# Attention scores image by image, gate values copied earlier, norm factors in one pass, and other dummy products on TensorE

## What is computed

```
h = concat(cls_tok, tokenizer(x))                    # [64, 6, 256]
h = h + gated_scan(layernorm(h))
h = h + ternary_linear(layernorm(h))
h = h + latent_attention(layernorm(h))
h = h + experts(layernorm(h))                        # 8 experts, top 48 tokens each
```

```
latent = x @ basis_w.T                                        # [B, T, 64]
lt     = einsum('btr,hrs->bhts', latent, head_mats)
att    = einsum('bhts,bus->bhtu', lt, latent) / sqrt(64)
att    = softmax(where(tril, att, -inf))                      # over the T keys of the same image
y      = (att @ v) @ o_w.T + o_b
```

## Time and profile of the kernel before

| | us |
|---|---|
| median of 3 runs | 232.57 (232.18 to 232.72) |
| profiled execution, its own time | 233.47 |
| span of its profile | 231.7 |
| PE busy, PEld busy | 218.0, 172.5 |
| DVE, ACT, POOL busy | 131.9, 73.8, 56.3 |
| mean granted clock of PE | 0.971 |

### The profile page before, as it was taken

How to read it: one execution, slowest core, us unless ns; L and a number is a source line. 1 busy time by engine, 2 the same in 40 slices (tenths; PEclk the granted TensorE clock), 3 DMA queues, 4 the chain that set the end, 5 groups by cost and what they waited for, 6 DMA issues and landing times.

```text
span 231.7 us, 3969 instructions
## 1 busy us (share of the span) xinstructions
PE 218.0 (94%) x1432; PEld 172.5 (74%) x1432; DVE 131.9 (57%) x419; ACT 73.8 (32%) x184; POOL 56.3 (24%) x122
## 2 busy tenths in 40 slices
PE   7999999999969999999999999999797899999995
PEld 5788888889958797778768867978676764655673
DVE  2597657576577475547865664864769525231212
ACT  2124242185676446013411621040036143130310
POOL 1043662266522123020232320300046150000000
PEclk9999999999999999859999997999999799999999
DMA  6999545940000000029999991000001204884002
GB/s 172 345 358 362 207 111 147 433 201 1 3 0 1 3 0 3 0 62 420 429 318 301 422 429 72 3 0 0 3 1 41 78 19 114 340 348 109 0 0 68
DMA packets 9747, 34.31 MB, mean 148 GB/s; under 512 B 1280, under 2 KB 3840, under 8 KB 7424
## 3 DMA queue, kind: packets, MB, share of 16 engines
q1 hardware_dynamic: 9728, 34.07, 40.9%
HBM read 32.88 MB, written 0.39 MB: 144 GB/s over the span
## 4 chain that ended last, share of the span: by engine, by line
PE 77%; DVE 9%; ACT 4%; issue 3%; POOL 3%; DMA 2%; SPq 2%; DVEq 0%; POOLq 0%; ACTq 0%
PE bank L451 16%; PE bank L1040 6%; PE bank L1014 6%; PE bank L676 5%; PE bank L685 5%; PE bank L575 4%; PE bank L600 3%; PE bank L553 3%; PE bank L743 2%; PE bank L440 2%; PE bank L982 2%; PE bank L755 2%; PE bank L463 2%; PE bank L1047 2%; DMA bench<-patches 2%
## 5 line engine op out<-in xcount | busy, mean ns | idle before, releaser
L451 PE MATMUL bank<-desk,bench 118*126 118x256 f32 x190 | 43.9, 381 | 0.2
L451 PEld LDWEIGHTS bank<-desk,bench 118*126 118x126 f32 x190 | 34.6, 188 | 6.2 <-DMA bench<-patches 0.9
L440 PE MATMUL bank<-zeros 128*128 128x256 f32 x94 | 28.2, 424 | 1.1 <-POOL small L1994 1.1
L1999 POOL TENSOR_TENSOR small<-small 96x2 f32<-96x2 f32 (+2 forms) x15 | 9.9, 659 | 70.5 <-DVE small L1312 51.3
L440 PEld LDWEIGHTS bank<-zeros 128*128 128x128 f32 x94 | 17.6, 206 | 3.9 <-POOL small L1994 1.1
L1747 ACT ACTIVATE attic<-bank,cols 128x126 f32<-128x126 f32 x38 | 15.2, 453 | 13.6 <-PE bank L463 13.4
L1094 DVE TENSOR_REDUCE bench<-bench 118x70 f32<-118x630 f32 x19 | 14.7, 798 | 6.5 <-DMA bench<-patches 6.4
L1740 ACT ACTIVATE desk<-bank 126x256 f32<-126x256 f32 x19 | 7.3, 384 | 25.7 <-PE bank L451 22.2
L2007 POOL TENSOR_TENSOR small<-small 126x1 f32<-126x1 f32 x19 | 10.5, 565 | 16.3 <-DVE small L1100 11.6
L685 PE MATMUL bank<-layw,bench 128*96 128x256 f32 x48 | 13.2, 424 | 1.4 <-DVE bench L1421 1.0
L676 PE MATMUL bank<-bench,layw 128*128 128x192 f32 x72 | 13.1, 331 | 0.5 <-ACT bench L1803 0.4
(11 more groups left out here) (220 smaller groups left out, 403.2 us busy)
## 6 DMA issues: line engine op xcount, KB each, us to landing
attic<-experts SPq DMA_DIRECT2D x10, 1024.0 KB, 8.1
desk<-experts SPq DMA_DIRECT2D x6, 1024.0 KB, 15.8
bench<-patches SPq DMA_DIRECT2D x19, 315.0 KB, 4.7
desk<-tokenizer_w SPq DMA_DIRECT2D x4, 576.0 KB, 5.9
layw<-layer_w SPq DMA_DIRECT2D x1, 2184.0 KB, 11.4
attic<-bias SPq DMA_DIRECT2D x8, 256.0 KB, 12.0
cons<-constants SPq DMA_DIRECT2D x1, 1258.0 KB, 5.5
desk<-conv_w SPq DMA_DIRECT2D x5, 128.0 KB, 3.6
```

What stands on the lines that cost most here:

```text
L440: mm(bank[b][:, 0:C], zeros[:, 0:P], zeros[:, :], start=True, stop=True)
L451: i = mm(conv_bank[t % 2][0:TP, 0:C], xt[t % XRING][0:KP, k, :], convw[0:KP, k, :], start=(k == 0), stop=(k == KX - 1))
L1999: pool.tensor_tensor(rs, var, half[0:parts, 0:rs.shape[1]], ALU.pow).then_inc(s(name), 1)
```

## The change

1. Scores image by image. There are 32 products per group, each for one image with its own keys: 48 stationary and 12 moving columns. Even images write partitions 0 to 47, odd ones 64 to 111 (`RH` = 64, `AR` = 112). Mask, softmax and weights have half the columns.
2. POOL makes the second norm's factors for both groups in one pass, `shift_both`. `norm_again` of either group waits for the whole pass.
3. ACT copies `valT` between `norm_again(0)` and `norm_again(1)`.
4. Dummies: one more at each of six places, two fewer at one.

```diff
-AR = 2 * NP2 * T
+RH = 64
+AR = RH + NP2 * T
...
-                        ("causal", 4 * T), ("slots", SW), ...
+                        ("causal", 2 * T), ("slots", SW), ...
...
-        att = [of_group(2 * GT + NP2 * GT + i * 2 * GT, GI // 2, 2, 2, T, parts=AR) for i in range(2)]
+        att = [of_group(2 * GT + NP2 * GT + i * 2 * GT, GI // 2, 2, T, parts=AR) for i in range(2)]
...
-        a_stat = carve(bench, o, 3, IMAGES * 2, parts=AR); o += 6 * IMAGES
+        a_stat = carve(bench, o, 3, IMAGES, parts=AR); o += 3 * IMAGES
...
+        of_image = lambda v, b: v[RH * b:RH * b + NP2 * T]
...
             def att_mask(g):
                 pe.wait_ge(s("lt_dve"), 2 * g + 1)
-                mm(bank[4 * g][0:AR, 0:2 * GT].rearrange("q (i n) -> q i n", n=4 * T), ident[0:AR, 0:AR],
-                   causal.unsqueeze(1).to_broadcast([AR, GI // 2, 4 * T]), start=True, stop=False, skip_group_check=True)
+                mm(bank[4 * g][0:AR, 0:GT].rearrange("q (i n) -> q i n", n=2 * T), ident[0:AR, 0:AR],
+                   causal.unsqueeze(1).to_broadcast([AR, GI // 2, 2 * T]), start=True, stop=False, skip_group_check=True)
...
-                for im in range(0, GI, 2):
-                    i = mm(bank[4 * g][0:AR, im * 2 * T:(im + 2) * 2 * T],
-                           ltT[g][:, im * T:(im + 2) * T, :], latD[g][:, im:im + 2, :, :], start=False, stop=True,
-                           skip_group_check=True)
+                for im in range(GI):
+                    at = im // 2 * 2 * T
+                    i = mm(of_image(bank[4 * g], im % 2)[:, at:at + 2 * T], ltT[g][:, im * T:(im + 1) * T, :],
+                           latD[g][:, im, :, :], start=False, stop=True, skip_group_check=True)
...
             local_back(0)
+            keep_warm(0, 1)
             turn_att(7)
...
             turn_att(8)
-            keep_warm(0, 2)
+            keep_warm(0, 3)
             global_spread(0)
...
             turn_x(0, 0)
+            keep_warm(4, 1)
             local_major(1)
...
             head_products(0)
-            keep_warm(7, 1)
+            keep_warm(7, 2)
             att_mask(0)
             att_scores(0)
             turn_x(1, 1)
             keep_warm(7, 1)
             ternary(1)
-            keep_warm(7, 2)
+            keep_warm(7, 3)
             spread_att(0, 0)
...
             att_scores(1)
             latent_out(0)
-            keep_warm(3, 3)
+            keep_warm(3, 1)
             spread_att(1, 0)
...
             pe.transpose(bank[4][:, 0:E8], cut_row, ident[0:E8, 0:E8]).then_inc(s("cut_turned"), 1)
-            keep_warm(3, 1)
+            keep_warm(3, 2)
...
-                act.wait_ge(s("again"), 5 * (g + 1))
+                act.wait_ge(s("again"), 5)
...
             norm_again(0)
+            act.wait_ge(s("vals_turned"), 1)
+            ac(valT, bank[5][:, 0:UT * E8].rearrange("p (t e) -> p t e", e=E8), ACT.Copy)\
+                .then_inc(s("valT_ready"), 1)
             norm_again(1)
             with_norm(1, 0)
             with_norm(1, 1)
-            act.wait_ge(s("vals_turned"), 1)
-            ac(valT, bank[5][:, 0:UT * E8].rearrange("p (t e) -> p t e", e=E8), ACT.Copy)\
-                .then_inc(s("valT_ready"), 1)
...
+            def shift_both():
+
+                mean, rs, nm = t_mv[0:TR, :, 0], t_rs[0:TR], t_nm[0:TR]
+                for g in range(G):
+                    pool.wait_ge(s(f"t_rs_ready{g}"), 4)
+                pool.tensor_tensor(t_sq[0:TR], rs, rs, ALU.mult).then_inc(s("again"), 1)
+                pool.wait_ge(s("again"), 1)
+                pool.tensor_scalar(t_again[0:TR], t_sq[0:TR], -EPS, 1.0 + EPS, ALU.mult, ALU.add)\
+                    .then_inc(s("again"), 1)
+                pool.wait_ge(s("again"), 2)
+                rsqrt(t_again[0:TR], t_sq[0:TR], "again", parts=TR)
+                pool.wait_ge(s("base_ready"), G)
+                pool.tensor_scalar(nm, mean, -1.0, None, ALU.mult).then_inc(s("nm_ready"), 1)
+                pool.wait_ge(s("again"), 3)
+                pool.tensor_tensor(t_s2[0:TR], rs, t_sq[0:TR], ALU.mult).then_inc(s("again"), 1)
+                pool.wait_ge(s("again"), 4)
+                pool.wait_ge(s("nm_ready"), G + 1)
+                pool.tensor_tensor(t_d2[0:TR], nm, t_s2[0:TR], ALU.mult).then_inc(s("again"), 1)
+                pool.tensor_scalar(t_up[0:TR], rs, 1.0, None, ALU.add).then_inc(s("up_ready"), G)
+                pool.tensor_tensor(t_dn[0:TR], nm, rs, ALU.mult).then_inc(s("shift_ready"), G)
...
-            rs_and_shift(3, 0, 1)
-            rs_and_shift(3, 1, 1)
+            shift_both()
```

More of the change, by code:

```diff
@@ L122 @@
 CONS, CONS_N = offsets([("ident", P), ("headcol", KC * H8), ("mask", TP), ("mask_cut", TP),
-                        ("causal", 4 * T), ("slots", SW), ("spread", 2 * T * P), ("heads8", KC * P), ("mean", P),
+                        ("causal", 2 * T), ("slots", SW), ("spread", 2 * T * P), ("heads8", KC * P), ("mean", P),
                         ("upto", P), ("all", P)])
@@ L1382, in heads_out @@
                                     bank[b][:, 0:2 * GT].rearrange("p (j n) -> p j n", j=2)).then_inc(s("lt_dve"), 1)
-            a3 = lambda i, g: att[i][g].rearrange("q i b p t -> q (i b p) t")
-            st = lambda i, g: a_stat[:, i, g * GI * 2:(g + 1) * GI * 2]
-            bc = lambda v: v.unsqueeze(2).to_broadcast([AR, GI * 2, T])
+            a3 = lambda i, g: att[i][g].rearrange("q i p t -> q (i p) t")
+            st = lambda i, g: a_stat[:, i, g * GI:(g + 1) * GI]
+            bc = lambda v: v.unsqueeze(2).to_broadcast([AR, GI, T])
             def att_shift(g):
-                scored = bank[4 * g][0:AR, 0:2 * GT].rearrange("q (i t) -> q i t", t=T)
+                scored = bank[4 * g][0:AR, 0:GT].rearrange("q (i t) -> q i t", t=T)
                 dve.wait_ge(s("att_scored"), g + 1)
@@ L2077, in rs_tokens, with rs_and_shift @@
                 rsqrt(t_mv[0:TR, sl, 1], t_rs[0:TR, sl], f"t_rs_ready{g}", parts=TR)
[L2079 removed]
+            def rs_and_shift(g):
                 sl = slice(TG * g, TG * (g + 1))
[L2082 to L2088, removed]
[L2089 to L2100 removed]
+                rs_tokens(0, g)
                 pool.tensor_scalar(t_nm[0:TR, sl], t_mv[0:TR, sl, 0], -1.0, None, ALU.mult).then_inc(s("nm_ready"), 1)
[L2102 to L2105 removed]
+                pool.wait_ge(s(f"t_rs_ready{g}"), 1)
+                pool.wait_ge(s("nm_ready"), g + 1)
                 pool.tensor_scalar(t_up[0:TR, sl], t_rs[0:TR, sl], 1.0, None, ALU.add).then_inc(s("up_ready"), 1)
@@ L2192, in _ @@
             probs(9)
-            rs_and_shift(0, 0, 0)
+            rs_and_shift(0)
             rs_local(1)
@@ L2197, in _ @@
             clear_latents(0)
-            rs_and_shift(0, 1, 0)
+            rs_and_shift(1)
             rs_tokens(2, 0)
@@ L2246, in constants @@
     at = np.arange(AR)
-    im, jt = at // (NP2 * T), at % (NP2 * T)
-    late = np.arange(T)[None, None, None] > (jt // NP2)[:, None, None, None]
-    other = np.arange(2)[None, :, None, None] != im[:, None, None, None]
-    causal = np.where(late | other, NEG, np.zeros((1, 1, 2, 1)))
+    im, jt = at // RH, at % RH
+    late = np.arange(T)[None, None] > (jt // NP2)[:, None, None]
+    causal = np.where(late, NEG, np.zeros((1, 2, 1)))
     chan = np.arange(P)
```

18 lines of the change are left out of this document (2 added, 16 removed).

## The result

The changed kernel took 225.65 us in the median of 4 runs (224.99 to 226.44), the kernel before 232.44 beside it (232.18 to 232.72): a ratio of 0.971, with an interval of 0.9675 to 0.9743. That is -6.8 us where -4.6 was forecast. The profiled execution of the changed kernel took 225.71 us.

A forecast was written before the change was run, and what follows sets the result against it. The prediction took TensorE, busy 94% of 231.7 us, as the bound, with three half-clock stretches. Terms -1.6 - 0.1 - 1.1 + 0.4 - 1.8 - 0.8 + 0.4 = -4.6, taken over to the median 232.57: 228.0 us, range 223.8 to 230.9.

The forecast's parts named there:

- all falls go: Rival: every half-clock stretch goes, at 96.6 and 182 us too, -2.2 and -1.5 more, 224.3 us; chance 0.20.
- Scores: Attention scores of both groups: 64 records at 0.030 us, 1.9 us for 2.7, -0.8 per group, -1.6 in all.
- the row of 32 columns: Scores: short weight loads of 32 columns, 0.030 us apart, taken as the price of a record.
- The prediction's own evidence against the rule: Experts' products of 128 rows on two sides of 64 columns: starts 0.01 us apart, 0.59 us both.
- Mask: Mask product of group 0, 192 moving columns for 384: -0.1 us; nothing in group 1, where it is hidden.
- Softmax: Group 1, between scores and spreads: DVE steps of half the size, 0.21 us less each, -1.1 us on the path.
- Ternary at full clock: Behind group 0's scores: the half-clock stretch at 141.0 us goes, ternary 1.74 us for 3.52, -1.8.
- Third dummy behind the ternary: Group 0, ahead of the spreads: one more dummy that no wait covers, +0.4 us.
- Early dummies: Three dummies in waits for DVE at 87 to 105 us: taken as 0, at most 0.1 us each.
- The end: Choosing the expert tokens: the cut row's turn no longer waits for `valT`, -0.8 us; second dummy ahead of the counts, +0.4.
- The clock: Of three places at half clock, the fall at 141.0 us goes, -1.8 us; those at 96.6 and 182.0 aren't counted.
- The slower rival: Scores: short records cost as much as long ones, 0.084 us each, 5.4 us per group, 235.0 us; chance 0.05.

The follow-up runs named there:

- the even-odd order: The changed kernel with the scores of all even images first, then all odd ones; median 233.24 us, ratio 1.002.
- the scores alone: The kernel before with scores image by image, mask and softmax of the change, old dummies and old order; median 227.98 us, ratio 0.986.
- the four variants: The changed kernel without early dummies (226.36 us), with two dummies behind the ternary (226.31), one ahead of the counts (227.83), or all old dummies (226.75).
- the two with filled waits: The changed kernel with two dummies behind the ternary and five more in waits, 225.07 us; the same with one dummy ahead of the counts, 225.07 us.
- one dummy ahead of the counts: The changed kernel with one dummy for two ahead of the counts; 227.83 us, ratio 0.984.

## Why the prediction was right, and where it was off

The direction, the terms of the path and the range held. But the 225.65 us lie nearer to the rival "all falls go" (224.3, with a chance of 0.20) than to the forecast of 228.0 (0.40): the path was right but for the size of the scores, the clock was not.

**Scores: right in kind, mis-sized.** -1.2 and -1.3 per group for -0.8. The sum took 0.030 us a record, from the row of 32 columns; what came is 0.0225 (32 pairs 0.045 us apart, the last with a tail of 0.17), at full clock in both groups:

```profile
135.82 1.61 PE L746 MATMUL bank<-bench 128*48 128x12 f32 x64 [0.21 <-DVE bench L1385]
```

The term that was mis-sized is this price of a record, chosen between two bounds. A pair takes one place of 0.045 us, which is what a single load of 48 columns takes in the even-odd order and is close to the 0.042 that I had by columns. Half of that, with full overlap, was 0.021: I had both figures and then chose a row of another kind because its width was nearer. The loads in the groups of forms:

```profile
L746 PEld LDWEIGHTS bank<-bench 128*48 128x48 f32 x128 | 3.1, 125 | 1.2 <-ACT bench L1845 1.2
```

128 loads are busy 3.1 us in all, at a mean of 125 ns each: most of each load lies over its neighbour. In the even-odd order the same loads, at the same mean, are busy 5.6 us:

```profile
L746 PEld LDWEIGHTS bank<-bench 128*48 128x48 f32 x128 | 5.6, 125 | 1.2 <-ACT bench L1845 1.2
```

The rule of the Trainium skill ("TensorE: Matmul & The Clock Gate", "Part 3: Packing small matmuls"), by which a weight load overlaps running products only where its row group is another one, doesn't hold here: all have 128 rows, and 1.61 us for 2.87, with loads busy 3.1 us for 5.6, is the overlap of two sides. The prediction's own evidence against the rule, was of two products and not of loads, and so was thinner than it said.

**Mask: right.** -0.1.

**Softmax: right.** -1.1 in group 1. The DVE steps took 0.35 us each, as taken:

```profile
L1394 DVE TENSOR_REDUCE bench<-bank 112x32 f32<-112x192 f32 x2 | 0.7, 357 | 3.6 <-PE bank L746 3.6
...
L1402 DVE RECIPROCAL bench<-bench 112x32 f32<-112x32 f32 x2 | 0.7, 354 | 0.1
```

That two dummies had to go for it is shown (+0.6 with three).

**Ternary at full clock: nearly.** 1.97 us for 3.52, -1.55, where the sum took 1.74 and -1.8.

**Third dummy behind the ternary: right.** +0.4, shown at both ends of its interval (5.78 and 5.34).

**Early dummies: right.** Nothing that shows (225.51 without, 225.49 with).

**The end: right.** Turn of the cut row -0.7 for -0.8, since the 0.14 us from the cut row to the turn, which the sum left out, stay; second dummy +0.4. The factors in one pass cost POOL 1.01 us for the power over four columns, and `valT` was copied at 169.56, 3.8 us ahead of the turn:

```profile
168.56 1.09 ACT L1865 ACTIVATE bench<-bench,small 96x256 f32<-96x256 f32 x2 [1.75 <-POOL small L2111]
169.56 0.17 ACT L1965 ACTIVATE small<-bank 128x24 f32<-128x24 f32 x1
...
172.97 0.21 DVE L1669 COPY bench<-small 8x128 f32<-8x128 f32 x1
173.33 0.20 PE L968 MATMUL bank<-cons,bench 8*128 8x8 f32 x1 [0.63 <-DVE bench L1669]
173.45 1.13 PE L442 MATMUL bank<-zeros 128*128 128x256 f32 x4
174.42 0.32 PE L972 MATMUL bank<-small,cons 128*128 128x48 f32 x2
```

PE's wait there is for DVE, the cut row, and no longer for ACT. Nothing behind it was late.

**The clock: the step that failed.** The sum read the places at half clock of one execution as a property of the kernel, one fall to go (-1.8) and two to stay. Two things were wrong in it. First, the number of stretches belongs to an execution: 0 to 4 for the kernel before, 2.2 in the mean, and the place changes (69, 97, 139 to 141, 164 to 169 and 173 to 182 us in the profiles of the variants). The profiled execution had four, and the median runs had about three; that is the 0.9 us between them of which I wrote that nothing in the trace says why. Second, the sum let the change reach only the fall behind the scores, while the half-clock stretches became rarer everywhere: the mean went from 2.2 to 0.4. The mean gain is 1.8 us, by accident the figure of the sum; beside the runs of the result it is 6.8 - 3.6 = 3.2. So of the 2.2 us by which the forecast was short, 0.8 are work and waits (-3.6 for -2.8 without the clock), the scores above all, and 1.4 the clock. These 1.4 are luck of the executions compared: mean against mean, over the 62 of before and the 9 of the changed kernel, the change is worth -5.4, not -6.8. In the profiled execution the rival "all falls go" is what happened, with the scores near their lower bound.

**What of the clock is shown, and what is open.** Shown: the scores bear on it (2.2 to 1.1 stretches with the scores alone, and 2.8 with the same records one after the other). Shown too: with the old scores the dummies don't help (2.2). That it is the light work which makes the clock fall fits both, but is argued and not shown; how it comes to a fall stays open. Open as well is what dummies add to the new scores. Without some or all of them the four variants had 16 stretches in 19 executions, the changed kernel 4 in 9, the two with filled waits 2 in 12. But the variant with two dummies more in group 1 had 3 in 5, no fewer than the changed kernel, so the order isn't simply that of more filling, and late moves of tokens ahead of the gathers are mixed into these numbers. Of the gain by the clock, then, the part of the scores is shown and that of the dummies is not settled.

The slower rival is out: it needed 0.066 us a record.

## What to carry to other kernels

Count the stretches at reduced clock in every execution before comparing two kernels, and compare executions with equally many: here 0 to 4 of them move the same kernel by 4.6 us, more than most edits are worth. Small products like these, with 48 stationary and 12 moving columns, should write alternate sides of the array, in neighbouring instructions; an order by side lost all of the gain (2.87 us for 1.61). A dummy belongs into a wait that is longer than it is, where it costs nothing; one with no wait behind it costs its full 0.43 us, so each needs a look at what it delays. Before a fall is put down to an edit, look at what PE waited for just ahead of it in that execution: here it was twice a transfer that landed late.

## What the runs showed of the hardware that I had not expected

- The same program has 0, 2, 3 or 4 stretches at 1.2 GHz per execution (13, 25, 10 and 14 of 62), never one, at 3.41 us each and 1.1 us of time each (233.70 less 229.11, by four).
- In the profiled execution of before, PE had no wait above 1.32 us ahead of any of the stretches; where the next one falls can't be read from one profile. In the variants one or two were common, so "never one" is of the kernel before.
- Two float32 products with 128 rows and 48 columns, on both sides of the array, run in the time of one: 64 records in 1.61 us, for 2.87 in the other order.
- SP's twelve moves of tokens from tile to tile landed within 1.8 to 2.2 us in ten of the fourteen profiles. In the other four the slowest took 3.4 (twice), 3.6 and 3.9 us, and in three of these PE waited for it ahead of the gathers, by 0.77, 1.55 and 1.85 us. In two of the three the clock fell right behind that wait (the scores alone, one dummy ahead of the counts), in the third it didn't. What makes a move late, no run shows.
